# Running maxima turned in blocks of neighbouring columns, and row maxima sent to DRAM one by one

## The reference, cut to what matters

```python
scores = jnp.einsum('hbnd,hbdm->hbnm', f_self, f_other)
masked = a_h * scores
masked = jnp.where(masked >= 0, masked, 0.2 * masked)
masked = masked / jnp.sqrt(jnp.float32(ATT))
masked = masked + jnp.where(a_h == 0, jnp.float32(-1000000000.0), jnp.float32(0.0))
attn = jax.nn.softmax(masked, axis=-1)
```

## Time and profile before

| | |
|---|---|
| median of 3 runs | 1936.47 us (1928.17 to 1937.74) |
| the profiled execution | 1936.72 us, span 1934.9 us |
| mean granted TensorE clock | 0.885 |
| busy, share of the span | PE 79%, PEld 37%, DVE 68%, ACT 64%, POOL 56% |
| instructions | 22052 |

### The profile page before, as it was taken

One profiled execution on the slowest core, in us unless ns is written; L12 is line 12 of the kernel. 1 busy time (PEld: TensorE's weight loads), 2 busy tenths in 40 slices (PEclk: granted clock), 3 DMA queues, 4 the chain that ended last, 5 costly groups with the idle time before them and its releaser, 6 DMA issues.

```text
span 1934.9 us, 22052 instructions
## 1 busy us (share of the span) xinstructions
PE 1521.3 (79%) x7728; PEld 725.5 (37%) x7728; DVE 1322.3 (68%) x1623; ACT 1242.3 (64%) x1475; POOL 1088.5 (56%) x581
## 2 busy tenths in 40 slices
PE   4588877887878788887888878787888877788655
PEld 2333333443334344343334433343443434334222
DVE  3667767776777677766787667776677667866554
ACT  2377767676767667675677667676676666776521
POOL 1065666655656555565565556566456655655642
PEclk9988888898899899998889998888888888898867
DMA  5413141302312042121413123120422204000000
GB/s 77 62 32 45 35 57 27 44 24 44 49 43 37 11 69 43 35 27 32 65 26 47 26 43 50 40 40 11 59 39 49 27 23 51 29 11 22 11 8 8
DMA packets 55067, 71.42 MB, mean 37 GB/s; under 512 B 21814, under 2 KB 42814, under 8 KB 54958
## 3 DMA queue, kind: packets, MB, share of 16 engines
q0 software_dynamic: 13824, 18.01, 12.5%
q1 hardware_dynamic: 41134, 52.01, 10.4%
HBM read 102.29 MB, written 3.26 MB: 55 GB/s over the span
## 4 chain that ended last, share of the span: by engine, by line
PE 45%; DVE 15%; ACT 15%; issue 14%; POOL 6%; SPq 2%; DMA 2%; ACTq 0%; POOLq 0%; DVEq 0%
PE M L535 11%; DVE RUN L823 9%; PE Z L496 8%; PE M L586 7%; ACT LS L677 7%; PE Z L498 7%; ACT LS L685 6%; PE Z L509 5%; POOL LS L403 5%; SPq L286 2%; PE Z L596 2%; PE Z L657 2%; POOL XP L412 2%; DMA MB<-row_maxima 1%; PE Z L552 1%
## 5 line engine op out<-in xcount | busy, mean ns | idle before, releaser
L403 POOL TENSOR_TENSOR LS<-LS,MB 125x1000 f32<-125x1000 f32 x384 | 887.9, 2328 | 672.1 <-DVE LS L837 520.7
L823 DVE TENSOR_TENSOR RUN<-Z,RUN 125x1000 f32<-125x1000 f32 x528 | 631.5, 1196 | 335.4 <-ACT LS L677 332.8
L677 ACT ACTIVATE LS<-Z 125x1000 f32<-125x1000 f32 x576 | 575.2, 999 | 250.0 <-PE M L535 173.9
L685 ACT ACTIVATE LS<-LS 125x1000 f32<-125x1000 f32 x576 | 594.7, 1034 | 39.6 <-POOL LS L403 26.8
L496 PE MATMUL Z<-AT,BI 126*125 126x500 fp8e4 x1152 | 399.3, 430 | 215.8 <-DVE RUN L823 171.3
L498 PE MATMUL Z<-FS,FO 96*125 96x500 bf16 x1152 | 372.8, 407 | 0.0
L535 PE MATMUL M<-LS,V 125*18 125x500 f32 x2304 | 350.5, 685 | 16.6 <-ACT LS L685 16.6
L496 PEld LDWEIGHTS Z<-AT,BI 126*125 126x125 bf16 x1152 | 140.3, 147 | 448.4 <-DVE RUN L823 278.3
L586 PE MATMUL M<-AT,XP 125*128 125x500 fp8e4 x756 | 211.7, 404 | 68.3 <-POOL XP L412 64.9
L837 DVE TENSOR_TENSOR LS<-LS,MB 125x1000 f32<-125x1000 f32 x192 | 244.9, 1276 | 4.0 <-DMA MB<-row_maxima 2.0
L498 PEld LDWEIGHTS Z<-FS,FO 96*125 96x125 bf16 x1152 | 170.2, 148 | 116.2 <-issue 30.2
(11 more groups left out here) (118 smaller groups left out, 1104.8 us busy)
## 6 DMA issues: line engine op xcount, KB each, us to landing
MB<-row_maxima SPq DMA_DIRECT2D x48, 488.3 KB
A<-in_adj_dram POOLq DMA_DIRECT2D x96, 183.1 KB, 4.7
FO<-PARTS SPq DMA_DIRECT2D x192, 46.9 KB, 2.1
FS<-PARTS SPq DMA_DIRECT2D x192, 46.9 KB, 2.1
XP<-in_x_dram SPq DMA_DIRECT2D x8, 375.0 KB
XA<-in_x_dram SPq DMA_DIRECT2D x8, 375.0 KB
out_dram<-X SPq DMA_DIRECT2D x7, 375.0 KB
row_maxima<-LMAX SPq DMA_DIRECT2D x48, 3.9 KB
```

Source lines behind the costliest of these rows:

```text
L403: nc.gpsimd.tensor_tensor(rows, rows, MB[:, u % 2, :, :], ALU.subtract).then_inc(sub_pool, 1)
L677: nc.scalar.activation(LS[:P, q % RL, :, :], banks("Z", q)[:P], ACT.Prelu, alpha=0.2).then_inc(bent, 1)
L685: nc.scalar.activation(rows, rows, ACT.Exp, scale=0.25).then_inc(exps, 1)
L823: nc.vector.tensor_tensor(run, z, run, ALU.max).then_inc(maxed, 1)
```

## The change

The transposes read RUN in blocks of 125 neighbouring columns, so that group c is the rows 125c to 125c + 124 of a head. A partition of LMAX then holds eight rows that lie 125 apart, and each goes to its own place in DRAM: 1000 pieces of 4 bytes. What DRAM holds after the write, and with it MB and everything later, is the same as before. The reduce, the bend, the waits and the broadcast are not changed.

```diff
@@ spread_maxima, on SP
-                sp.dma_start(spread[u % 2].rearrange("(h i c) -> i h c", i=P, c=ST),
-                             LMAX[:, u % 2, :].rearrange("p (h c) -> p h c", c=ST)).then_inc(max_out[u % 2], 16)
+                sp.dma_start(spread[u % 2].rearrange("(j i) -> i j", i=P), LMAX[:, u % 2, :],
+                             allow_slow_non_contiguous=True).then_inc(max_out[u % 2], 16)
@@ turn_run, on TensorE
                 for hh in range(2):
                     for c in range(ST):
-                        last = nc.tensor.transpose(z[:P, hh, c * P:(c + 1) * P], RUN[:, u % 2, hh, c:C:ST], ID[:P, :P])
+                        last = nc.tensor.transpose(z[:P, hh, c * P:(c + 1) * P], RUN[:, u % 2, hh, c * P:(c + 1) * P], ID[:P, :P])
```

## The result

The changed kernel takes 1985.9 us (1979.7 to 1997.3, 4 runs) against 1937.1 us: a ratio of 1.027, interval 1.021 to 1.033. It is 49 us **slower**. The forecast was 34 us faster, with 1934 us as the top of the range. The profiled execution is the longest of the four, 1997.3 us (span 1995.5 us).

What follows compares the result with a forecast made beforehand. A chain hopping between engines was taken to bound the kernel, with the transposes on it. Gain 46 us, costs 3.6 and 8.4 us: -34 us from 1936.7, so 1903 us, range 1885 to 1934 us.

Steps and rivals of the forecast that it cites:

- What bounds the kernel: No engine is full; a chain hopping between engines sets the time, with 94.8 us of it on line 509's transposes.
- Part one, duration: Line 509's eight transposes, read without a step, take 1.08 us a turn instead of 2.10, 1.02 us less.
- Part one, 46 us: Gain from line 509's shorter transposes wherever the chain passes them: 94.8 x 1.02/2.10 = 46 us.
- Rival 1: Smaller gain, 1911 to 1927 us: turn takes 1.4 us, ScalarE stalls count fully, or half turns at low clock; chance 0.16.
- part two: Row maxima written to DRAM as 1000 pieces instead of 250: costs 3.6 us outright plus 8.4 us of ScalarE stalls.
- Part two, "150 x 8 ns = 1.2 us later": The maxima's DRAM write: 150 more packets on each of five engines, 8 ns each, end it 1.2 us later.
- rival 3: Single elements cost more than 16-byte packets; waiting for MB replaces the transposes; slower, 1962 us at X = 5; chance 0.10.
- Part two, what lateness costs: Late MB: 3.6 us outright, and 16.8 us of ScalarE stalls in 14 units, half reaching the end, 8.4 us.
- the formula of rival 3: Cost of late MB, half the stalls counted: 17X - 14 us, equal to 46 us gain at X = 3.5.
- X: Extra microseconds one write of the maxima takes; 3.5 us corresponds to 23 ns per packet over one engine's 150.
- the 10 us bound: Upper end for the write's added time, from the whole queue's mean packet of 78 ns: 150 x 69 ns.

Runs made afterwards that it cites:

- e2_write_only: Kernel before with only the DRAM write changed to 1000 pieces of 4 bytes, transposes keeping their step: 2034.3 us, ratio 1.052.

## Why the prediction was wrong

- **What bounds the kernel:** right. The transposes were on the chain, and taking them alone off it made the kernel faster.
- **Part one, duration:** right. Loads of 189 ns for the 188 taken, and a turn of 1.11 us at full clock for 1.08. Of the Trainium skill's two rules that were weighed, that of the 16-byte line (SBUF — State Buffer, Door 1) held, and that of the column count (TensorE: Matmul & The Clock Gate, Part 2, LDWEIGHTS) did not: the same 125 columns took 325 and 189 ns.
- **Part one, 46 us:** too high; alone it gave 27. Of the chain's 94.8 us 40 came off, because 14 of the 48 turns fall wholly or in part at the low clock, where a dense turn is hardly shorter. Rival 1 had this mechanism, with half the turns. With the step the clock did not show in the length, so the earlier trace rows should have been weighed against how often TensorE is at the low level at a turn. For the rest the runs show longer stalls of ScalarE (14 us more), of which the sum had some booked under part two, and a slightly lower granted clock; how it splits between them stays open.
- **Part two, "150 x 8 ns = 1.2 us later":** this is the step that failed. The price per packet was right, 9 ns, and the packets ended about 1 us later. But the sum treated the rest of the write, 1.3 of 1.71 us, as a constant. It is not. SP's wait came to 6.46 us, 4.75 more and not 1.2, and in the write shown the stretch from the last packet to the semaphore grew from 0.6 to 4.1 us. The probes show that this stretch depends on how small the pieces are and how they lie in DRAM. The rows of before had only one layout, so the range should have let that part grow as well as the packets'. The argument held against rival 3, that a packet costs little whatever it carries, was about engines and not about completion.
- **Part two, what lateness costs:** the formula of rival 3 at X = 4.75 gives 17 x 4.75 - 14 = 67 us, and the runs 79. For the step kept (no gain of 1 us for the consumers) it gives 3X + 7(X - 1) + 7(X - 2) = 59 us at 4.7, and e2_write_only measured 100. So letting only half of the stalls reach the end was too kind. Two reasons are seen but not priced: after the stall of unit 24 TensorE ran on at the low clock, and subtractions of VectorE and GpSimd that run side by side take longer, 32 and 28 us in all. Neither was in the sum.
- **Rivals:** rival 3 had the right step, a wait for MB that takes the place of the transposes, and came near in size, 1962 us at X = 5 against 1986, with a chance of 0.10 and outside the range. It put the extra time on the packets, 23 ns each at the point where gain and cost are equal, and there it was not: they took 9 ns. By its own formula, the point of X = 3.5 us was in sight of the 10 us bound that part two itself named, so its chance was too low. The figure of the Trainium skill for packets (DMA: Bandwidth & Descriptors, Measured) put the write 7.9 us later as an estimate. Measured were 4.75 us, a little nearer to that than to the 1.2 us of the sum, but by luck: the packets, whose price it is, ended only about 1 us later.

## What to carry to other kernels

A DMA's cost has three parts: issue, packets, and the time until completion is told; packets cheap in the first trace say nothing of the third, which many small pieces written side by side in DRAM lengthened most here. Before changing the order in which values are written, look for an order that is good on both sides: here pairs, two f32 to a 16-byte line for every engine that reads with a step and 32 contiguous bytes for the write, took both gains. And the price of lateness is not even: where half the units already waited for MB, double the lateness cost over three times as much, 95 against 28 us.

## What the runs showed of the hardware

- The same 4000 bytes from 125 partitions, written to DRAM by SP with nothing else running: as 1000 single words 7.1 to 7.3 us where they touch, 3.9 us at a pitch of 8 bytes and 3.6 us at 64 or 128 (a partition's eight words side by side at a pitch of 8: 7.1 us, with slower packets); as 500 pieces of 8 bytes 3.8 to 3.9 us touching and 2.35 us at a pitch of 64; as 16-byte pieces 2.0 us touching and 1.76 us spaced; as 125 pieces of 32 bytes 1.4 us. The packets of the 4-byte layouts with a pitch of 4 and of 64 end at the same 2.1 us.
- A weight load of 125x125 f32 takes 189 ns dense, 196 ns at two words to 16 bytes and 325 ns at one. VectorE's subtraction with one operand at one word in 32 bytes takes 2.0 us instead of 1.19, GpSimd's 2.81 instead of 2.32. VectorE's subtraction of 1.19 us took up to 3.3 us beside one of GpSimd's. VectorE's maximum with RUN read and written at a step of 500 bytes takes 1.95 us instead of 1.20.
- The dense transposes depend on the clock, 1.11 us for eight at 2.4 GHz and 2.04 us at 1.2 GHz. Those with the step took 2.06 us (unit 16) with a granted clock of 1.00 over the window, 2.08 us (unit 18) with 0.60 and 2.19 us (unit 4) with 0.50: the length of these hardly follows the clock.
